# Loading and splitting the first expert's weights in the routing stage, asking for the first corners earlier, and moving the corner masks of a turn

## What is computed

```
logits = ((x @ wt.T) + repeat(g @ wg.T)) / 2
scores = softmax(logits);  topk_w = two largest of a token, normalized to sum 1
for each expert e:  y_e = (leaky(x @ w_gate[e]) * (x @ w_up[e])) @ w_down[e]
y = sum over the token's two experts of topk_w * y_e
y = y + (leaky(x @ sw_gate) * (x @ sw_up)) @ sw_down
x = x + y
```

## Time and profile before

| | us |
|---|---|
| median of three runs | 2171.32 |
| lowest and highest run | 2169.38, 2174.14 |
| the profiled execution's own time | 2168.78 |
| its span, from first to last instruction | 2166.6 |
| TensorE busy (matmul) | 1955.9 (90%) |
| VectorE busy | 1659.9 (77%) |
| ScalarE busy | 1345.3 (62%) |
| GpSimd busy | 1044.4 (48%) |
| mean granted TensorE clock | 0.948 of full speed |

### The profile page before, as it was taken

One profiled execution on the slowest core, in us unless ns is written; L12 is line 12 of the kernel. 1 busy time (PEld: TensorE's weight loads), 2 busy tenths in 40 slices (PEclk: granted clock), 3 DMA queues, 4 the chain that ended last, 5 costly groups with the idle time before them and its releaser, 6 DMA issues. The chain is left out here.

```text
span 2166.6 us, 39267 instructions
## 1 busy us (share of the span) xinstructions
PE 1955.9 (90%) x12122; PEld 1437.1 (66%) x12122; DVE 1659.9 (77%) x4092; ACT 1345.3 (62%) x2921; POOL 1044.4 (48%) x1309
## 2 busy tenths in 40 slices
PE   5999496999999998589999999985796999999988
PEld 4888464666666668466666666675564666666668
DVE  4787856888888886657888887858567888888857
ACT  2222566677777774247777776744575777777753
POOL 0443213566766662305666665624024666766633
PEclk8999698899999999898999999997797999999999
DMA  3731068333333343386888888841466433333333
GB/s 108 213 111 47 2 233 299 91 120 120 119 120 120 120 152 115 104 294 201 246 252 251 249 253 253 249 155 46 123 226 201 132 117 118 118 117 118 118 117 117
DMA packets 248074, 339.38 MB, mean 157 GB/s; under 512 B 28694, under 2 KB 154780, under 8 KB 247868
## 3 DMA queue, kind: packets, MB, share of 16 engines
q1 hardware_dynamic: 247868, 336.86, 49.7%
HBM read 250.62 MB, written 102.91 MB: 163 GB/s over the span
## 5 line engine op out<-in xcount | busy, mean ns | idle before, releaser
L1698 POOL TENSOR_SCALAR at_row<-at_row,at_inv 128x769 f32<-128x769 f32 (+7 forms) x384 | 696.6, 1814 | 413.0 <-DVE at_inv L1854 411.5
L1897 ACT ACTIVATE at_row<-at_row,at_nmax 128x769 f32<-128x769 f32 (+7 forms) x768 | 595.3, 775 | 217.8 <-DVE at_nmax L1871 210.4
L1871 DVE CUSTOM_DVE_ANT_0 at_row<-at_s,bias,at_row 128x768 f32<-128x768 f32 (+7 forms) x768 | 614.4, 811 | 56.3 <-PE at_s L1802 33.5
L1814 PE MATMUL at_t<-ident,at_row 128*128 128x128 f32 x3456 | 530.1, 281 | 2.2 <-ACT at_pt L1892 1.5
L1814 PEld LDWEIGHTS at_t<-ident,at_row 128*128 128x128 f32 x3456 | 390.1, 141 | 206.4 <-issue 111.3
L1801 PE MATMUL at_s<-k_hh,q_hl 128*128 128x512 f32 (+3 forms) x1152 | 461.3, 401 | 33.9 <-SPq L1762 23.0
L1829 PE MATMUL at_o<-at_pt,v 128*64 128x256 f32 (+3 forms) x2688 | 455.7, 455 | 1.7 <-DVE at_pt L1709 1.7
L1802 PE MATMUL at_s<-k_lp,q_h 65*128 65x512 f32 (+3 forms) x1152 | 393.2, 353 | 0.0
L1892 ACT ACTIVATE at_pt<-at_t 128x512 f32<-128x512 f32 (+2 forms) x576 | 309.3, 537 | 116.5 <-PE at_t L1814 114.4
L1709 DVE COPY at_pt<-at_t 128x384 f32<-128x384 f32 (+3 forms) x576 | 281.1, 488 | 114.7 <-PE at_t L1814 113.9
L1829 PEld LDWEIGHTS at_o<-at_pt,v 128*64 128x64 f32 x2688 | 161.0, 136 | 161.3 <-issue 96.9
(11 more groups left out here) (253 smaller groups left out, 2811.5 us busy)
## 6 DMA issues: line engine op xcount, KB each, us to landing
q_dram<-o_in SPq DMA_DIRECT2D x76, 512.0 KB, 3.9
bias<-bands_dram SPq DMA_DIRECT2D x64, 512.0 KB, 5.8
q_hl<-q_dram SPq DMA_DIRECT2D x96, 256.0 KB, 4.2
q_hl<-q_dram SPq DMA_DIRECT2D x192, 128.0 KB, 3.1
bands_dram<-brow_dram SPq DMA_DIRECT2D x2, 8192.0 KB, 32.2
bias<-corners_dram SPq DMA_DIRECT2D x256, 64.0 KB, 4.7
bias<-in_fside SPq DMA_DIRECT2D x32, 448.0 KB, 4.1
q_h<-q_dram SPq DMA_DIRECT2D x48, 256.0 KB, 4.9
```

The costliest lines, as they stand in the source:

```text
L1698: return eng.tensor_scalar(cells(u), cells(u), inv[:, u % RING:u % RING + 1], None, ALU.mult)
L1814: last = eng.transpose(t_ps[m % NTR][:, c * P:(c + 1) * P], weights(u)[:, here:here + P], t["ident"][:])
L1871: eng.tensor_tensor_reduce(out=weights(u), in0=s_ps[u % 2][:, 0:width], in1=bt[:, lo:lo + width], scale=-1.0, scalar=null_cell(u)[:, 0:1], ...
L1897: eng.activation(cells(u), cells(u), ACT.Exp, scale=-1.0, bias=nmax[:, i:i + 1], accum_out=rsum[:, i:i + 1]).then_inc(s["exp"], 1)
```

## The change

Routing gets the weight buffers (`moe_raw`, `moe_wh`, `moe_wl`, now allocated outside both stages, so that they live through both). Behind its other loads SyncE asks for the three pieces of unit 0's weights, waits for them, does the same for unit 1's and waits again. ScalarE copies unit 0's weights to `moe_wh` behind its copy of `ebc` and ahead of the exponential. GpSimd makes `moe_wl` of unit 0. At the start of the expert stage nothing is loaded or split for unit 0 (only the 16 factors are copied), and TensorE's increment comes at once; unit 1's weights are there and its split stays behind chunk 2. SyncE asks for the four corners of turn 0 first, then for the inputs of the next stages. The four masks of a turn stand behind the chunks 1, 3, 4 and 5.

```diff
--- before.py
+++ after.py
@@ -243,13 +243,27 @@
-def moe_route(nc, t, x, wt_t, cond_t, wg_t):
+EXPERTS_AT_ONCE = 2
+EXPERT_COLS = 2 * KD * M + D
+
+
+def load_expert(eng, t, sem, weights, unit, q):
+
+    w_gate, w_up, w_down = weights
+    one = bass.ds(unit, 1)
+    for src, at in ((w_gate, 0), (w_up, KD * M)):
+        eng.dma_start(t["moe_raw"][:, q, at:at + KD * M].rearrange("p (k m) -> p k m", k=KD),
+                      src[one, :, :].rearrange("o (k p) m -> p (o k) m", p=P)).then_inc(sem, 16)
+    eng.dma_start(t["moe_raw"][:, q, 2 * KD * M:], w_down[one, :, :].rearrange("o p d -> p (o d)")).then_inc(sem, 16)
+
+
+def moe_route(nc, t, x, wt_t, cond_t, wg_t, experts):
     CH = B * S // BANK
     TPC = NTT // CH
     NTR = 4
     names = ["w_in", "x_tr", "x_hi", "x_lo", "w_hl", "cond_mm", "lt", "lt_copy", "logits", "dve", "exp_in", "exp_out"]
-    names += [f"x_in{c}" for c in range(CH)] + ["select_in"]
+    names += [f"x_in{c}" for c in range(CH)] + ["select_in", "first_in", "second_in", "first_hi", "first_lo"]
     with tensors(nc) as (sb, ps):
         ebc = sb("route_ebc", [P, NPAIR + 1, P])
         wt = sb("route_wt", [P, KD, E])
@@ -287,6 +301,9 @@
                                   ).then_inc(s[f"x_in{c}"], 16)
                 eng.dma_start(t["esel"][:], t["in_esel"]).then_inc(s["select_in"], 16)
                 eng.dma_start(ebc[:], t["in_ebc"]).then_inc(s["select_in"], 16)
+                for q, name in enumerate(("first_in", "second_in")):
+                    load_expert(eng, t, s[name], experts, q, q)
+                    eng.wait_ge(s[name], 48)
                 eng.wait_ge(s["w_in"], 80)
                 for c in range(CH):
                     eng.wait_ge(s[f"x_in{c}"], 16)
@@ -334,8 +351,17 @@
                                    tr[n % NTR].rearrange("p (k i) -> p k i", k=KD), ACT.Copy).then_inc(s["x_hi"], 1)
                 eng.wait_ge(s["select_in"], 48)
                 eng.activation(t["ebc"][:], ebc[:], ACT.Copy)
+                eng.wait_ge(s["first_in"], 48)
+                eng.activation(t["moe_wh"][:, 0, :], t["moe_raw"][:, 0, :], ACT.Copy).then_inc(s["first_hi"], 1)
                 eng.wait_ge(s["exp_in"], 1)
                 eng.activation(score[:], shifted[:], ACT.Exp).then_inc(s["exp_out"], 1)
+
+            @block.gpsimd
+            def _(eng):
+                eng.wait_ge(s["first_hi"], 1)
+                eng.tensor_tensor(t["moe_wl"][:, 0, :], t["moe_raw"][:, 0, :], f32(t["moe_wh"][:, 0, :]), ALU.subtract
+                                  ).then_inc(s["first_lo"], 1)
+                eng.wait_ge(s["first_lo"], 1)
             @block.vector
             def _(eng):
@@ -411,17 +437,16 @@
 def moe_experts(nc, t, w_gate, w_up, w_down, fside, inputs):
     NC = 4
-    PAR = 2
+    PAR = EXPERTS_AT_ONCE
     TURN = PAR * NC
     TPC = NTT // NC
-    WC = 2 * KD * M + D
     RUN = (NU // PAR, TURN, 2, 2)
     CORNERS = H // (NU // PAR - 1)
+    MASKS_AT = (1, 3, 4, 5)
     names = ["w_in0", "w_in1", "w_split", "w_hi", "gu", "slope", "leaky", "hidden", "hid_hi", "hid_lo", "down",
              "added"] + [f"corner_{n}{j}" for n in ("in", "masked", "out") for j in range(CORNERS)]
     with tensors(nc) as (sb, ps):
-        raw = sb("moe_raw", [P, PAR, WC])
-        wh, wl = (sb(f"moe_w{n}", [P, PAR, WC], FR) for n in "hl")
+        raw, wh, wl = (t[f"moe_{n}"] for n in ("raw", "wh", "wl"))
         slope = sb("moe_slope", [P, 2, BANK])
         leaky = sb("moe_leaky", [P, 2, BANK])
         hid = sb("moe_hid", [P, 2, BANK])
@@ -439,14 +464,6 @@
         marks = dict(w_split=PAR, gu=TURN, slope=TURN, w_hi=2 * PAR, leaky=TURN, hidden=TURN, hid_hi=TURN, hid_lo=TURN,
                      down=TURN, added=TURN)
         with Phase(nc, t, names) as (block, s):
-            def load(eng, unit, q):
-                one = bass.ds(unit, 1)
-                for src, at in ((w_gate, 0), (w_up, KD * M)):
-                    eng.dma_start(raw[:, q, at:at + KD * M].rearrange("p (k m) -> p k m", k=KD),
-                                  src[one, :, :].rearrange("o (k p) m -> p (o k) m", p=P)).then_inc(s[f"w_in{q}"], 16)
-                eng.dma_start(raw[:, q, 2 * KD * M:WC],
-                              w_down[one, :, :].rearrange("o p d -> p (o d)")).then_inc(s[f"w_in{q}"], 16)
-
             @block.sync
             def _(eng):
                 def load_corners(it, j):
@@ -463,16 +480,17 @@
                 for j in range(CORNERS):
                     eng.sem_inc(s[f"corner_out{j}"], 16)
                 for q in range(PAR):
-                    eng.wait_ge(s["w_split"], q + 1)
-                    load(eng, q, q)
+                    eng.sem_inc(s[f"w_in{q}"], 48)
+                for j in range(CORNERS):
+                    load_corners(0, j)
                 load_inputs(eng, t, *inputs)
                 for it in range(NU // PAR - 1):
                     turn = Turns(s, it, marks)
-                    for j in range(CORNERS):
+                    for j in range(CORNERS if it else 0):
                         load_corners(it, j)
                     for q in range(PAR):
                         turn.wait(eng, "w_split", q + 1)
-                        load(eng, it * PAR + (PAR + q), q)
+                        load_expert(eng, t, s[f"w_in{q}"], (w_gate, w_up, w_down), it * PAR + (PAR + q), q)
                     for j in range(CORNERS):
                         store_corners(it, j)
                 for q in range(PAR):
@@ -547,8 +565,8 @@
                 for it in range(NU // PAR - 1):
                     for c in range(TURN):
                         low_hidden(it, c)
-                        if 1 <= c <= CORNERS:
-                            mask_corners(it, c - 1)
+                        if c in MASKS_AT:
+                            mask_corners(it, MASKS_AT.index(c))
                 for c in range(TURN):
                     low_hidden(NU // PAR - 1, c)
@@ -557,6 +575,12 @@
                 def split(turn, it, unit):
                     q = unit % PAR
+                    if it * PAR + unit == 0:
+                        eng.sem_inc(s["w_split"], 1)
+                        eng.sem_inc(s["w_hi"], 1)
+                        eng.tensor_copy(unit_w[:, q, :], t["expert_w"][:, 0, :]).then_inc(s["w_hi"], 1)
+                        eng.wait_ge(s["w_hi"], 2 * PAR + 2)
+                        return
                     eng.wait_ge(s[f"w_in{q}"], it * 48 + 48 * (unit // PAR + 1))
                     turn.wait(eng, "down", (unit - PAR + 1) * NC)
                     turn.wait(eng, "added", (unit - PAR + 1) * NC)
@@ -2265,7 +2289,11 @@
             t["xt_h"] = sb0("xt_h", [P, KD, NTT * P], FR)
             t["xt_l"] = sb0("xt_l", [P, KD, NTT * P], FR)
             t["expert_w"] = sb0("expert_w", [P, NU, NTT])
-            moe_route(nc, t, a["x"].rearrange("b s d -> (b s) d"), a["wt_t"], a["cond_t"], a["wg_t"])
+            t["moe_raw"] = sb0("moe_raw", [P, EXPERTS_AT_ONCE, EXPERT_COLS])
+            for part in "hl":
+                t[f"moe_w{part}"] = sb0(f"moe_w{part}", [P, EXPERTS_AT_ONCE, EXPERT_COLS], FR)
+            moe_route(nc, t, a["x"].rearrange("b s d -> (b s) d"), a["wt_t"], a["cond_t"], a["wg_t"],
+                      (a["w_gate"], a["w_up"], a["w_down"]))
             moe_experts(nc, t, a["w_gate"], a["w_up"], a["w_down"], a["fside"], inputs_of(1))
         for layer in (0, 1, 2, 3):
             w = inputs_of(layer)[0] if layer else None
```

## The result

The changed kernel took 2154.85 us (median of six runs, 2152.14 to 2158.61), the kernel before 2170.35 (six runs beside them). The ratio is 0.9934, with a 95% interval of 0.9916 to 0.9951: 15.5 us less, faster by 0.7%. Its profiled execution took 2156.53 us, with a span of 2154.7 us, against 2168.78 and 2166.6: 12 us less.

What follows compares the result with a forecast made beforehand. TensorE was taken to set the expert stage's pace, so only its waits counted: 5.3 + 1.45 - 0.1 + 2.75 = 9.4 us off the median 2171.32 gave 2161.9 us, range 2158.8 to 2166.2.

Steps and rivals of the forecast that it cites:

- Base: Time of the kernel before from which the forecast gain was subtracted: 2171.32 us, the median of the runs shown.
- The sum: Expert stage's gains added, 5.3 + 1.45 - 0.1 + 2.75 = 9.4 us, with no stage after it changed.
- TensorE's clock: Expert stage's start: clock is down at an earlier start too, 4.9 us of slow running come again; no gain.
- The start: Expert stage's start: TensorE begins at 33.7 instead of 38.98 us, 5.3 us gained, bounds 5.0 and 5.6.
- rival (c): First chunk of the expert stage: 2.4 GHz granted sooner after shorter idle time, 2.4 us more, 2159.5 us; chance 0.06.
- part 1: First expert's weight load and split move into routing, so TensorE starts the expert stage earlier: 5.3 us gained.
- Part 2: Turn 0: first corners asked for ahead of next inputs; GpSimd's wait goes, 1.45 us gained, 0.1 given back.
- Part 3: Turns 1 to 3: masks behind chunks 1, 3, 4, 5 stop holding VectorE's copy, 3 x 0.92 = 2.75 us gained.
- the 2.5 us to spare: Mask behind chunk 5 ends at 104.8 us, before the cast of chunk 6 at 107.32, so it is harmless.
- Cover in routing: Added DMAs, ScalarE's copy (0.8 us) and GpSimd's subtraction (1.9 us) end over 7 us before routing does, costing nothing.
- Rival (b): Routing: GpSimd's new subtraction holds VectorE's chain, 1.9 us lost, 2163.8 us; chance 0.09.

Runs made afterwards that it cites:

- idle products: Changed kernel plus 32 TensorE products of 512 columns behind routing's last transposes, into an unread buffer: mean 2154.8 us over eleven runs, ratios 0.9932 and 0.9936.
- five subtractions: Changed kernel with GpSimd's new subtraction in routing made five times in a row instead of once: 2157.66 us in one run.
- the delay: Changed kernel with VectorE filling an unread buffer 34 times at routing's end: ratio 0.9998 (0.9988 to 1.0008), mean 2168.0 us.
- part 1 alone: Changed kernel with corners again after the inputs and masks behind 1, 2, 3, 4, keeping the first weights' load and split in routing: ratio 0.9981.

## Why the prediction was wrong in its number

Two steps failed: the base from which the sum was subtracted, and the term for TensorE's clock, put at nothing.

**Base.** This is the largest error. The sum was subtracted from 2171.32, the median of three runs. All 112 runs of the kernel before have a mean of 2168.7 (22 at 2167.6 and 90 at 2169.0). The prediction allowed 2 us either way for the median of a few runs; the base alone was 2.6 to 3.7 too high.

**The start (5.3 us, bounds 5.0 to 5.6): right.** 5.1 in the profiled pair; over the traces 39.1 (three of before) against 33.7 (five of after), 5.4.

**TensorE's clock (no gain, rival (c) with 2.4 us and a chance of 0.06): wrong step.** That "the 4.9 us of slow running come again" did not come true. Before, 12 or 13 products run at the low level, in three traces; after, 7 to 9, in five. The row of the changed kernel that answers to rows 5, and the next:

```profile
33.90:37.20 3.30, 3.30 (x8) 2.62 (x9) 0.17 (x1) 0.00 (x0) 0.00 (x0) 0.50 0.70 187
37.30:40.00 2.70, 2.70 (x12) 2.13 (x12) 0.69 (x1) 0.60 (x1) 0.00 (x0) 0.97 1.15 286
```

The level is 1.2 GHz up to 37.2 us and nearly full after that. A slow product takes 0.43 us from start to start and a fast one 0.23, so five fewer are 1.0 us. Rival (c) named the place, but its reason, the shorter idle time, is not shown. Leaving out the two traces with idle products, all kernels without part 1 (six traces) have 11 to 13 slow products and all with it (ten) 7 to 9. After 9.3 us of idle time there are 7 to 9, after 12.3 us 9 (the kernel with five subtractions), after 14.1 to 14.4 us 11 to 13, but after 22.6 us (the delay) 7 again. Even with 9.3 us each time, the stages that start at 33.3 to 33.4 us have 7 and those at 33.6 to 33.9 us 8 or 9. So the moment of the start may count as well, and the cause stays open.

**Part 2 (1.45 us, less 0.1): right, with a gap in the reasoning.** The cast of expert 1 went from 0.55 to 0.97 us as said, and its split ends at 49.76, where TensorE starts the unit at 49.81, 0.31 us after the product before it instead of 0.12: a loss of 0.2 us where 0.1 was given back. Expert 2's weights are asked for at 54.05 (53.8 forecast) and split at 64.88 (65.3 forecast), with no new wait. What the text did not see is that part 2 is worth 1.45 us only without part 1. With it, the wait that it removes has grown to 4.2 us and takes the clock down besides. The sum came out right because it was made for the three parts together.

**Part 3 (2.75 us): right,** 2.6 us alone in the kernel before and 3.6 us as the difference that it makes within the changed kernel, where turn 0 would be a fourth such turn. The mask behind chunk 5 is harmless, as the 2.5 us to spare said, and one behind chunk 6 is not.

**Cover in routing: right.** Rival (b) did not come about, but its mechanism is real and reaches further than the prediction's rows: had the weights landed after 26 us or so instead of before 15.6, GpSimd's subtraction would have met two-input operations and, by the experiment with five subtractions, could have held one of them for 1.5 us.

**The sum.** 9.4 us were forecast; 10.3 are in the traces and 10.9 in the times. Of the 7.1 us between 2161.9 and 2154.85, 3.7 are the base (to 2167.6), 0.9 the traced gain, 0.6 what the times have beyond the traces, within their error, and 1.9 the first six runs, whose median lies that far under the mean of all 28. The last term is luck. The base alone would not have saved the forecast: from 2167.6 it is 2158.2, with a low end of 2155.1, still above 2154.85; with the clock's 1.0 us besides, the measured time would have lain inside. The range was too narrow since it took the scatter of the forecast kernel's median alone: the base's and the new kernel's add up. For the sizes at hand the scatter of the later stages, 5.2 us in one layer with the same code, is as large as each part of this change.

## What to carry over

When a change starts a stage earlier, look for each wait in that stage whose end is set by something that does not move with it, here a DMA behind 25 others in a queue: whatever part of the gain that something does not follow goes into the wait, so its present length (1.4 us) understates what removing it is worth (4.2 us, and 1.6 more since TensorE's clock fell behind it). When two engines slow each other, find the pair of instructions by their common end, and move the one that is free to move to where the other does not stand; moved to the next split, it costs the same again. And for a gain of half a per cent take the mean of many runs of the kernel before, not the median of three, as the base of the sum.

## What the hardware showed unexpectedly

- GpSimd's subtraction held two of VectorE's operations with two SBUF inputs until its own end, 1.77 us instead of 0.29, not only copies (1.06 instead of 0.16). The holding goes both ways: the mask took 1.41 us instead of 1.09 when it came up beside VectorE's cast.
- After the idle time TensorE ran slow for 3.0 to 5.7 us, with 7 to 13 slow products, and the fewest after both the shortest and the longest idle time (9.3 and 22.6 us). With 32 idle products up to 31.5 us and 1.8 us of idle time it stayed fast.
- With part 1 alone, TensorE's clock was at its full level for a microsecond after a stop of 4.2 us and only then fell to the low one, for 3.3 us; after a stop of 1.4 us it did not fall.
